# Which engine issues the two transfers of the maxima rows: SyncE before, ScalarE after

## The reference, cut to what matters

```python
h = _layernorm(x) * (1 + ca) + sa
q, k, v = (h @ W.T  split into 8 heads, for W in (Wq, Wk, Wv))
scores = einsum('bhqd,bhkd->bhqk', q, k) / scale      # scale = hd ** 0.5
scores = where(causal, scores, -inf)
x = x + ga * (softmax(scores) @ v)
h = _layernorm(x) * (1 + cb) + sb
x = x + gb * _L0_ffn_ref(h, gate_W, expert_W, out_W)
```

## Time and profile before

| | |
|---|---|
| time, median of 3 runs | 302.49 us (302.0 to 303.42) |
| the profiled execution: span from first to last instruction | 300.6 us |
| difference of the two | 1.89 us |
| TensorE busy (matmul) | 273.2 us, 91% |
| VectorE busy | 214.6 us, 71% |
| ScalarE busy | 198.0 us, 66% |
| GpSimd busy | 50.5 us, 17% |
| DMA moved | 11.25 MB, mean 37 GB/s |
| granted TensorE clock, mean | 0.969 |

### The profile page before, as it was taken

One profiled execution on the slowest core, in us unless ns is written; L12 is line 12 of the kernel. 1 busy time (PEld: TensorE's weight loads), 2 busy tenths in 40 slices (PEclk: granted clock), 3 DMA queues, 4 the chain that ended last, 5 costly groups with the idle time before them and its releaser, 6 DMA issues.

```text
span 300.6 us, 5682 instructions
## 1 busy us (share of the span) xinstructions
PE 273.2 (91%) x2043; PEld 124.5 (41%) x2043; DVE 214.6 (71%) x413; ACT 198.0 (66%) x409; POOL 50.5 (17%) x83
## 2 busy tenths in 40 slices
PE   7999965997799999999999999999999998998943
PEld 2555631433335444434334433334445544444412
DVE  3867772899998999989988997889998702031033
ACT  2476473480377878658776686776677698988920
POOL 6953021050030320110010200020011002010020
PEclk9799995999999999999999999999999999999995
DMA  7105693029830049900000010000000100000000
GB/s 205 39 9 149 64 113 33 0 91 129 98 34 2 2 143 125 120 4 0 2 1 3 0 35 2 1 4 0 2 1 2 35 4 2 0 20 1 2 0 19
DMA packets 14094, 11.25 MB, mean 37 GB/s; under 512 B 1290, under 2 KB 13922, under 8 KB 14066
## 3 DMA queue, kind: packets, MB, share of 16 engines
q1 hardware_dynamic: 13490, 10.36, 22.0%
q10 hardware_dynamic: 576, 0.53, 0.5%
HBM read 7.34 MB, written 3.41 MB: 36 GB/s over the span
## 4 chain that ended last, share of the span: by engine, by line
PE 70%; DVE 8%; DMA 5%; ACT 4%; issue 3%; SPq 2%; POOL 0%; POOLq 0%; ACTq 0%; DVEq 0%
PE ctx_ps L964 22%; PE ps L926 19%; PE ps L942 17%; DVE part_max L710 6%; DMA k_stack<-piece_scratch 5%; PE ps L1044 2%; PE ps L979 2%; PE ps L948 2%; ACT probs L610 2%; SPq L497 2%; PE ps L1013 1%; PE ps L1039 1%; PE ps L1008 1%; PE ps L1033 1%; ACT h_t L675 1%
## 5 line engine op out<-in xcount | busy, mean ns | idle before, releaser
L610 ACT ACTIVATE probs<-ps 128x512 f32<-128x512 f32 (+3 forms) x312 | 153.4, 546 | 53.1 <-PE ps L926 49.9
L710 DVE TENSOR_REDUCE part_max<-ps 128x2 f32<-128x1024 f32 (+3 forms) x160 | 163.4, 1058 | 22.0 <-PE ps L942 16.0
L942 PE MATMUL ps<-k_stack,q_stack 112*128 112x512 bf16 (+3 forms) x320 | 85.0, 352 | 10.2 <-DMA k_stack<-piece_scratch 5.5
L926 PE MATMUL ps<-q_stack,k_stack 114*128 114x256 bf16 (+3 forms) x432 | 91.6, 303 | 0.6 <-ACT h_t L675 0.2
L964 PE MATMUL ctx_ps<-probs,v_aug 128*32 128x256 f32 (+3 forms) x864 | 79.9, 449 | 0.4 <-POOL probs L583 0.3
L926 PEld LDWEIGHTS ps<-q_stack,k_stack 114*128 114x128 bf16 x432 | 36.4, 98 | 56.2 <-ACT probs L610 33.8
L583 POOL TENSOR_SCALAR_AFFINE_SELECT probs<-probs 128x512 f32<-128x512 f32 x32 | 20.3, 638 | 166.0 <-ACT probs L610 165.9
L942 PEld LDWEIGHTS ps<-k_stack,q_stack 112*128 112x128 bf16 x320 | 26.8, 99 | 46.7 <-DVE part_max L710 17.6
L964 PEld LDWEIGHTS ctx_ps<-probs,v_aug 128*32 128x32 f32 x864 | 18.0, 108 | 27.6 <-ACT probs L610 16.4
L823 DVE RECIPROCAL sum_inv<-ps 128x16 f32<-128x16 f32 (+1 forms) x10 | 2.3, 229 | 34.8 <-PE ps L1033 34.8
L536 POOL TENSOR_TENSOR rstd<-var_eps,half_neg 128x4 f32<-128x4 f32 (+1 forms) x9 | 8.5, 949 | 67.2 <-DVE var_eps L736 67.2
(11 more groups left out here) (93 smaller groups left out, 166.2 us busy)
## 6 DMA issues: line engine op xcount, KB each, us to landing
q_stack<-piece_scratch SPq DMA_DIRECT2D x21, 128.0 KB, 5.8
k_stack<-piece_scratch SPq DMA_DIRECT2D x21, 128.0 KB, 6.2
piece_scratch<-piece SPq DMA_DIRECT2D x9, 256.0 KB, 2.3
x_sb<-in_L_attn_hidden_states SPq DMA_DIRECT2D x4, 256.0 KB, 4.7
out_x<-result SPq DMA_DIRECT2D x3, 256.0 KB, 2.3
wmod<-in_L_wmod ACTq DMA_DIRECT2D x1, 384.0 KB, 4.3
out_x<-result SPq DMA_DIRECT2D x2, 128.0 KB, 2.0
q_stack<-max_row SPq DMA_DIRECT2D x12, 4.0 KB
```

Of the source, the lines that this page charges most:

```text
L610: drained(act.activation(probs[:, b % PROB_BUFS, heads * e:heads * e + heads, q0:tiles * P], bank.rearrange("p (h q) -> p h q", h=heads)[: ...
L710: dve.tensor_reduce(part_max[:, n % 2, i, 2 * e:2 * e + 2, c], banks[:, :, 0:width], AX.X, ALU.max).then_inc(vec_drained, 1)
L926: last = pe.matmul(bank[:, m * tiles * P + q0:(m + 1) * tiles * P], k_stack[0:rows, h, j * P:(j + 1) * P], q_stack[0:rows, h, tile * P + q ...
L942: last = pe.matmul(banks[:, m, 0:width], q_stack[0:ROWS, h, tile * P:(tile + 1) * P], k_stack[0:ROWS, h, c * BANK:c * BANK + width], start ...
```

## The change

The transfers move from SP's stream to ACT's. ACT waits until its own copy to `max_row` has been written, issues the two transfers, and goes on. In the planner's costs, `max_t` loses its 1200 ns of SP and has 680 ns of ACT in place of 480. All other code is the same.

```diff
-        "max_t": (220, [("act", 480), ("sp", 1200)], ROWS_TO_SCORES),
+        "max_t": (220, [("act", 680)], ROWS_TO_SCORES),
...
@@ sync engine
-                elif step[0] == "max_t":
-
-                    n = step[1]
-                    (tile, tiles), first = BLOCKS[n // 2], HALF * (n % 2)
-                    sp.wait_ge(act_drained, act_slot[step] + 1)
-                    for a in range(SHIFT_ROWS):
-                        sp.dma_start(q_stack[ROWS + a:ROWS + a + 1, first:first + HALF, tile * P:(tile + tiles) * P],
-                                     max_row[HALF * a:HALF * (a + 1), n % 2, 0:tiles * P]).then_inc(max_in[n], 16)
...
@@ scalar engine
-                    tiles = BLOCKS[n // 2][1]
+                    (tile, tiles), first = BLOCKS[n // 2], HALF * (n % 2)
                     rows = bank.bitcast(BF16)[0:SHIFT_ROWS * HALF, 0:tiles * P]
                     drained(act.copy(max_row[:, n % 2, 0:tiles * P], rows))
+                    act.wait_ge(act_drained, act_slot[step] + 1)
+                    for a in range(SHIFT_ROWS):
+                        act.dma_start(q_stack[ROWS + a:ROWS + a + 1, first:first + HALF, tile * P:(tile + tiles) * P],
+                                      max_row[HALF * a:HALF * (a + 1), n % 2, 0:tiles * P]).then_inc(max_in[n], 16)
```

## The result

The changed kernel takes 325.27 us (324.2 to 326.38, 4 runs) against 302.96 us for the one before on the same chip (302.0 to 303.69): a ratio of 1.075, 95% interval 1.0706 to 1.0794, 22 us slower. The forecast was 299.3 us.

What follows compares the result with a forecast made beforehand. It took TensorE as the bound from 92 us, VectorE from 53 to 92, with an idle stretch at 44 to 49. Restart -3.6, clock -1.7, stops +2.15 took 302.49 to 299.3 us; range 296.9 to 304.0.

Steps and rivals of the forecast that it cites:

- What bounds the kernel, and the strips: Group 1's strips, late through SP's wait and limited by DMA engines, would be usable at 44.4 us, 4.4 us earlier.
- The sum: Restart -3.6, clock -1.7 and ACT stops +2.15 us: -3.15 us in all, from 302.49 to 299.3 us.
- Item 0's first scores can't come earlier: Item 0's rows would be issued by about 37.4 us as now, so its first scores stay at 39.06 us.
- The rival for this: Item 0's rows are held by the strips and land at 44.4 instead of 39 us; 305.1 us in all; chance 0.07.
- At item 2 I had let VectorE, the bound there, cover any wait: At item 2, if scores are placed sooner, PE has VectorE to wait for anyway; nothing was counted.
- A rearranged order can give or take about 1 us anywhere, for which I take 0: Anywhere in the kernel, the planner's new order of steps could shift time by about 1 us; counted as 0.
- the term of 0 to 0.66 us that I had for the strips of group 2: SP's wait until 76.58 us goes too, but VectorE bounds there and PE waits only 0.66 us; counted 0.
- The stops: ACT waits and issues two transfers at ten items, 1.26 us each; behind item 0 costing 2.15 us, bounds 0 and 7.6.
- The clock: PE work from 49 to 53 us, at half clock, would run at the upper level: 1.7 us won, up to 2.0.
- Two of the signs of being wrong: PE waiting for max_row's transfers near 39 or 79 us; a stretch where the new order alone loses over 2 us.

Runs made afterwards that it cites:

- e1: The changed kernel with the planner's old costs: ACT issues the rows, every engine's order of steps is that of the kernel before; 313.07 us, ratio 1.0335.
- e4: The kernel before, no ACT issue; SP puts the rows of items 0 and 2 behind the last strips of groups 1 and 2; 310.59 us, ratio 1.0243.
- e2: The kernel before, SP issuing the rows, with only the changed kernel's planner costs of max_t and so its order; 317.13 us, ratio 1.0474.
- e9: e2 with the stream that prepares groups 2 and 3 preferred by 800 ns in the planner; 307.38 us, ratio 1.0154.
- e10: The kernel before with old costs; SP issues the rows of items 0 to 2, ACT those of items 3 to 9; 305.34 us, ratio 1.0115.
- e11: The changed kernel, with SP waiting until the rows of items 0 and 2 have landed before it issues further strips; 323.51 us, ratio 1.0694.
- e7: The kernel before with two strip steps (four transfers) behind item 0's rows issued ahead of them by SP; 299.2 us, ratio 0.9879.

## Why the prediction was wrong

**What bounds the kernel, and the strips: right.** The strips were late through SP's wait and limited by the DMA engines. Without the wait SP issues them in one run, and in e1 they end near 43.9 us; I had said 42.6 and a landing at 44.4. The sum is added up rightly from its terms; the terms below are what failed.

**"Item 0's first scores can't come earlier" (and, as was assumed with it, not later): wrong.** I let the rows be usable at 39 us with strips in flight until 42.6. The rival for this had 0.07, because one of ACT's transfers had landed in 2.8 us amid the loads of x; that row was from another state of the queues and was no measure of eight or more strips ahead. The rival's mechanism is what happened, twice and not once: 8.01 and 7.98 us. In the old order it costs 8.0 us (e4), with the wait of 4.86 us that goes already taken off; the rival had priced it at 2.65 us over the time before, for item 0 alone. At item 2 I had let VectorE, the bound there, cover any wait. It did not: from 53 to 92 us VectorE is busy 30.92 us in the changed kernel, against 37.21.

**"A rearranged order can give or take about 1 us anywhere, for which I take 0": wrong, and the largest miss.** e2 measures it: 14.5 us. I had seen only that scores and maxima move by 1.25 us in the plan, and took the list behind to shift with them. It doesn't: here group 2's preparation fell back by 20 steps of the list. That moves the eight strips that stood ahead of item 2's rows behind them, and PE waits 5.90 us for the strips; the term of 0 to 0.66 us that I had for the strips of group 2, and took at nothing, failed with it. Some 4 us of the 14.5 come late, between items 6 and 7, and stay open (e9).

**The stops: right in mechanism, small in size.** For items 3 to 9 I had 1.65 us (0.6 + 0.3 + 0.4 + 0.25 + 0.1); e10 has 2.74 us, item 3 alone 1.07, where ACT's first pair took 1.82 us in place of 1.20. In the changed order they cost more: from item 2's context copy to item 9's, the changed kernel (130.33 to 310.06 us) takes 3.2 us longer than e2 (126.59 to 303.11 us), with the same order and the rows issued by SP.

**The clock: the gain became a loss.** I expected 1.7 us back because the gap of 4.86 us would close. It grew to 8 us and a second one came, with a clock of 0.50 behind each: PE is busy 7.4 us longer for as many matmuls, where I had forecast about 2 us less. How much of this reaches the time was not taken apart; it is contained in what e1, e2 and e4 measure.

**The sum.** By the start of item 9's context copy the changed kernel is 22.0 us behind (310.06 against 288.02). e2 is 15.1 us behind: that is the order. The other 6.9 us are ACT's issue in that order: 2.9 us by item 1, 0.8 more by item 2, and 3.2 us of stops. The first two are differences of single executions in a stretch where e10 differed by 1.6 us without a change; the distances from item 2 on agree to 0.01 us between the kernel before and e4. In the old order the same issue costs 10.6 us (e1): the rows' two waits hurt less in the changed one since, as e11 shows, strips would be waited for there anyway.

The Trainium skill (DMA: Bandwidth & Descriptors, section Issuing engines are not separate DMA queues) has transfers of different engines run on the same 16 DMA engines and interleave. The first half is what the runs bear out: rows from ACT's queue were as late as rows from SP's own (45.59 and 46.74 us). Interleaving in the sense that a small transfer passes a backlog on the other queue does not show: 637 packets of SP's queue and none of ACT's in five microseconds (e1). The measurement decides.

Two of the signs of being wrong that the prediction named are what came: PE waiting for the rows of items 0 and 2, and the new order alone losing over 2 us.

## What to carry to other kernels

Moving a small urgent transfer to another issuing engine does not lift it over bulk transfers already issued: in this kernel what counted was how much had been issued ahead of it, on either queue. An in-order wait in front of bulk transfers can be the thing that keeps them out of the way; before it is removed, work out what then lies ahead of whom, and hand the DMA engines only what they can finish in the time until the urgent transfer. Where a planner's costs are changed together with the code, time the new costs alone: here they alone cost 14.5 us, two thirds of the loss.

## What the runs showed that I had not expected

- The order of issue holds across the two queues, and it is not a wait for idle engines. For item 2 of the changed kernel eight strips had been issued ahead of the first row transfer and ten ahead of the second. The DMA engines took none of ACT's packets from 83 to 89 us, 8 between 89 and 90, 8 between 90 and 91, and strips went on until 96 us: the four strips issued later were not waited for. The rows were usable at 92.99 us, 2.1 us after their last packet had ended; at the other waits this was 1.4 to 1.7 us. Whether ACT's packets stood back in the DMA engines or before they reached them, no run shows.
- ACT's first pair of row transfers took 1.8 us in each of the five kernels that have it (1.82, 1.81, 1.82, 1.82, 1.81), most later ones 1.2 us.
- In e7 PE stood still for 2.96 us until 42.27 us. The granted clock was 0.84 at 40 us, still within the gap, and 0.50 from 41 to 47 us, while PE was busy without a break from 43 us on; in the kernel before, a gap of 0.66 us at 87 us was followed by 1.00.

```profile
43.00:44.00 1.00, 1.00 (x5) 0.51 (x4) 0.04 (x1) 0.49 (x1) 0.00 (x0) 0.50 1.01 101
44.00:45.00 1.00, 1.00 (x3) 0.29 (x2) 1.00 (x1) 0.61 (x2) 0.00 (x0) 0.50 0.26 20
```
